# Two graph-attention blocks on one core: x's transposes between the first chunks, and four changed orders

## What is computed

```python
def gat_conv(x, src, dst, W, a_src, a_dst, b, heads, out_ch):
    h = (x @ W).reshape(n, heads, out_ch)
    e = leaky_relu(alpha_src[src] + alpha_dst[dst], 0.2)   # alpha = sum(h * a)
    p = exp(e - segment_max(e, dst)[dst])
    alpha = p / segment_sum(p, dst)[dst]
    return segment_sum(h[src] * alpha, dst) + b
```

## Time and profile before

| what | us |
|---|---|
| median of 3 runs | 380.62 (380.08 to 380.71) |
| the profiled execution, its own time | 379.96 |
| its span | 378.2 |
| PE busy | 357.7 (95%) |
| PEld busy | 306.3 (81%) |
| POOL busy | 248.1 (66%) |
| DVE busy | 218.0 (58%) |
| ACT busy | 214.8 (57%) |
| DMA | 65.15 MB, mean 172 GB/s |

### The profile page before, as it was taken

One profiled execution on the slowest core, in us unless ns is written; L12 is line 12 of the kernel. 1 busy time (PEld: TensorE's weight loads), 2 busy tenths in 40 slices (PEclk: granted clock), 3 DMA queues, 4 the chain that ended last, 5 costly groups with the idle time before them and its releaser, 6 DMA issues.

```text
span 378.2 us, 6192 instructions
## 1 busy us (share of the span) xinstructions
PE 357.7 (95%) x2103; PEld 306.3 (81%) x2106; DVE 218.0 (58%) x563; ACT 214.8 (57%) x374; POOL 248.1 (66%) x171
## 2 busy tenths in 40 slices
PE   6999888999999999999999999998789999899992
PEld 2888787988988988898898898897567888688882
DVE  3697777318236345543741832836665787944866
ACT  4993458756665664773765665564553657245501
POOL 2777707776946948749668686690459876577911
PEclk9999999999999999999999999999999999999998
DMA  7967944637527545754662753755253365355002
GB/s 266 346 193 231 332 196 122 224 124 256 190 87 221 201 160 168 220 194 117 218 240 91 250 170 111 248 184 164 64 188 110 88 179 172 146 168 167 2 0 83
DMA packets 24544, 65.15 MB, mean 172 GB/s; under 512 B 1952, under 2 KB 3024, under 8 KB 24528
## 3 DMA queue, kind: packets, MB, share of 16 engines
q1 hardware_dynamic: 20720, 55.19, 44.4%
q10 hardware_dynamic: 3808, 9.76, 8.1%
HBM read 64.15 MB, written 0.79 MB: 172 GB/s over the span
## 4 chain that ended last, share of the span: by engine, by line
PE 72%; ACT 7%; DVE 6%; issue 6%; POOL 4%; DMA 3%; SPq 1%; POOLq 0%; ACTq 0%; DVEq 0%
PE ps L908 51%; PE ps L1151 8%; PE ps L999 6%; POOL ring_lo L360 3%; ACT ring_hi L347 2%; PE ps L1017 2%; DMA x_sb<-in_x 2%; DMA raw<-in_L_gnn_W 2%; PE ps L972 1%; PE ps L1212 1%; ACT rows_hc L684 1%; POOL x_sb L613 1%; ACT z L684 1%; ACT am L684 1%; PE ps L958 1%
## 5 line engine op out<-in xcount | busy, mean ns | idle before, releaser
L360 POOL TENSOR_TENSOR ring_lo<-raw,ring_hi 128x768 fp32r<-128x768 f32 x94 | 170.8, 1852 | 78.5 <-ACT ring_hi L347 78.5
L347 ACT ACTIVATE ring_hi<-raw 128x768 fp32r<-128x768 f32 x96 | 77.5, 851 | 32.6 <-PE ps L908 28.6
L376 POOL TENSOR_TENSOR ring_lo<-raw,ring_hi 128x512 fp32r<-128x512 f32 (+1 forms) x40 | 59.7, 1523 | 30.6 <-ACT ring_hi L369 30.6
L1341 DVE CUSTOM_DVE_ANT_0 e<-ps,att 128x768 f32<-128x768 f32 (+1 forms) x56 | 41.9, 801 | 53.7 <-PE ps L908 51.1
L908 PE MATMUL ps<-ring_hi,zT_hi 128*128 128x512 f32 (+1 forms) x256 | 69.4, 346 | 1.1 <-DVE zT_lo L1497 1.1
L908 PE MATMUL ps<-ring_hi,zT_lo 128*128 128x512 f32 (+1 forms) x256 | 67.4, 338 | 0.0
L908 PE MATMUL ps<-ring_lo,zT_hi 128*128 128x512 f32 (+1 forms) x256 | 67.3, 338 | 0.0
L908 PE MATMUL ps<-ring_hi,xT_hi 128*128 128x512 f32 x192 | 51.8, 346 | 0.1
L908 PE MATMUL ps<-ring_lo,xT_hi 128*128 128x512 f32 x192 | 51.0, 342 | 0.0
L908 PE MATMUL ps<-ring_hi,xT_lo 128*128 128x512 f32 x192 | 50.6, 340 | 0.0
L908 PEld LDWEIGHTS ps<-ring_lo,zT_hi 128*128 128x128 f32 x256 | 43.1, 188 | 5.7
(11 more groups left out here) (157 smaller groups left out, 554.0 us busy)
## 6 DMA issues: line engine op xcount, KB each, us to landing
raw<-in_L_gnn_W SPq DMA_DIRECT2D x54, 768.0 KB, 4.4
raw<-in_L_gnn_Wr SPq DMA_DIRECT2D x8, 768.0 KB, 4.4
att<-in_L_gnn_a_src ACTq DMA_DIRECT2D x10, 384.0 KB, 4.5
att<-in_L_gnn_a_dst ACTq DMA_DIRECT2D x10, 384.0 KB, 5.5
raw<-in_L_gnn_W SPq DMA_DIRECT2D x4, 384.0 KB, 5.6
x_sb<-in_x SPq DMA_DIRECT2D x3, 256.0 KB, 5.2
rows_hc<-in_L_gnn_b SPq DMA_DIRECT2D x1, 512.0 KB, 5.8
rows_hc<-in_L_gnn_g SPq DMA_DIRECT2D x1, 512.0 KB, 6.7
```

The costliest lines, as they stand in the source:

```text
L347: eng.activation(slot_hi(c), raw_chunk(c), ACT.Copy).then_inc(hi_done, 1)
L360: eng.tensor_tensor(slot_lo(c), raw_chunk(c), slot_hi(c).bitcast(F32), ALU.subtract)\
L376: eng.tensor_tensor(ring_lo[:, q["ring_at"]:q["ring_at"] + w], raw[:, q["raw_group"], q["raw_at"]:q["raw_at"] + w], ring_hi[:, q["ring_at" ...
L1341: dve.tensor_tensor_reduce(junk[:, at:at + w], of[:, (k - first_head(a)) * w:(k - first_head(a) + 1) * w], att[:, half_at * row + k * w:ha ...
```

## The change

It touches all five orders named above. (1) x's parts 1 and 2 are transposed by PE between chunks 0 and 1 and between chunks 1 and 2, and PE's wait for `xT_lo` stands behind them. ACT copies part 1 after it has split chunk 2, and part 2 after the self-loop ramps and the split of chunk 3. DVE writes four hots before `input_lo(1)` and four before `input_lo(2)`. (2) In head 0's ELU the ReLUs of pair 2 come ahead of the high part of pair 1. (3) conv2's exponentials come ahead of the attention loads and of a chunk split, and two idle matmuls are gone. (4) Tile 0 of h1 is centred, scaled and half of it added before tile 1's second statistics. (5) At the end the centring and shift of both tiles come before the first addition.

```diff
@@ act: the opening @@
+            def input_hi(b):
                 act.wait_ge(xT_ps, b + 1)
                 act.activation(xT_hi[:, 2 * b:2 * b + 2, :].rearrange("p k n -> p (k n)"),
                                ps[:, XT_AT + b * BANK:XT_AT + (b + 1) * BANK], ACT.Copy).then_inc(xT_hi_done, 1)
+            split_hi(act, FIRST_PHASE, 0, reused=False)
+            input_hi(0)
+            split_hi(act, FIRST_PHASE, 1, reused=False)
+            split_hi(act, FIRST_PHASE, 2, reused=False)
+            input_hi(1)
             act.wait_ge(iota_cast, 2)
             act.wait_ge(self_cast, 1)
             ramps(ET, ET + NT)
             split_hi(act, FIRST_PHASE, 3, reused=False)
+            input_hi(2)
@@ act: elu(h, hi_first) @@
-                    if q >= 1 and hi_first:
-                        elu_hi(h, q - 1)
+                    if q == 1 and hi_first:
+                        elu_hi(h, 0)
...
-                    if q >= 1 and not hi_first:
+                    if q == 2 or q == 1 and not hi_first:
                         elu_hi(h, q - 1)
@@ act: conv2 @@
             projected_tile_hi(A_CONV2, 1)
+            exps(A_CONV2, (0, 1))
+            chunks_hi(2, 3)
             load_att(A_GAT1A, b1_as1.rearrange("h c -> (h c)"), b1_ad1.rearrange("h c -> (h c)"), HC)
-            chunks_hi(2, 3)
-            exps(A_CONV2, (0, 1))
             weights_tiles_hi(A_CONV2)
@@ pe: the opening @@
+            transpose_x(0)
             for c in range(CH):
-                if c % 2 == 0:
-                    pe.wait_ge(xT_lo_done, c // 2 + 1)
                 if c == 1:
                     pe.wait_ge(b1_loaded, 16)
                     pe.transpose(...)
+                if c in (1, 2):
+                    transpose_x(c)
+                if c % 2 == 0:
+                    pe.wait_ge(xT_lo_done, c // 2 + 1)
                 project_chunk(FIRST_PHASE, 0, c, at=ACC)
@@ pe: conv2 @@
             weights_tiles(A_CONV2)
-            keep_warm(2, idle)
             aggregate(A_CONV2)
@@ dve: the opening @@
             split_lo(dve, FIRST_PHASE, 0)
             input_lo(0)
             split_lo(dve, FIRST_PHASE, 1)
-            input_lo(1)
...
+            hots(0, 4)
+            input_lo(1)
+            hots(4, 8)
             input_lo(2)
...
+            hots(8, ET)
@@ dve: h1 @@
             biased_half(1, 0)
             layer_mean(1, 0, 3 * NT + 1)
-            biased_half(1, 1)
-            layer_mean(1, 1, 3 * NT + 2)
             h1_centre(0, 0)
             h1_centre(1, 0)
             h1_scale(0, 0)
             h1_add(0, 0)
             h1_scale(1, 0)
+            biased_half(1, 1)
+            layer_mean(1, 1, 3 * NT + 2)
+            h1_lo(0, 0)
             h1_centre(0, 1)
-            h1_lo(0, 0)
             h1_centre(1, 1)
             h1_scale(0, 1)
             h1_add(0, 1)
+            h1_add(1, 0)
             h1_scale(1, 1)
-            h1_add(1, 0)
             h1_lo(0, 1)
@@ dve: the end @@
+            out_stats(0)
+            out_centre(0)
+            out_stats(1)
+            out_shift(0)
+            out_centre(1)
+            out_shift(1)
+            for i in range(NT):
                 dve.wait_ge(out_shifted, i + 1)
                 parts = (slice(0, D),) if i == 0 else (slice(N, D), slice(0, N))
```

More of the change, by code:

```diff
@@ L684, in ramps @@
                     act.activation(ramp(t), iota[:, :], ACT.Relu, bias=bias).then_inc(ramp_act_done, 1)
-            split_hi(act, FIRST_PHASE, 0, reused=False)
-            for b in range(3):
+            def input_hi(b):
                 act.wait_ge(xT_ps, b + 1)
@@ L690, in _ @@
                                ps[:, XT_AT + b * BANK:XT_AT + (b + 1) * BANK], ACT.Copy).then_inc(xT_hi_done, 1)
-                if b < 2:
-                    split_hi(act, FIRST_PHASE, b + 1, reused=False)
+            split_hi(act, FIRST_PHASE, 0, reused=False)
[3 more added lines that the diff above has]
+            input_hi(1)
             act.wait_ge(iota_cast, 2)
@@ L1024, in _, with transpose_x @@
             pe.wait_ge(consts, 2)
-            for b in range(3):
+            def transpose_x(b):
                 pe.wait_ge(x_loaded[b], 16)
@@ L1306, in _, with hots @@
             dve.tensor_copy(ident_b, ident[:, :]).then_inc(ident_cast, 1)
+            def hots(first, end):
+                for t in range(first, end):
+                    dve.tensor_scalar(hot(t, 1), iota_ps, edges_f[:, 1, t:t + 1], None, ALU.is_equal)\
+                       .then_inc(hot_done, 1)
+                    if t >= ACT_RAMPS:
+                        dve.tensor_scalar(ramp(t), iota_ps, edges_f[:, 0, t:t + 1], 0.0, ALU.add, ALU.max)\
+                           .then_inc(ramp_dve_done, 1)
             split_lo(dve, FIRST_PHASE, 0)
@@ L1315, in _ @@
                .then_inc(ramp_biased, 1)
+            dve.wait_ge(iota_cast, 1)
+            dve.wait_ge(ramp_biased, 1)
+            hots(0, 4)
+            input_lo(1)
+            hots(4, 8)
             input_lo(2)
@@ L1712, in _, with out_stats, out_centre @@
             nat = [ps[:, GAT2_NAT_AT[i]:GAT2_NAT_AT[i] + D] for i in range(NT)]
-            for i in range(NT):
+            def out_stats(i):
                 dve.wait_ge(nat_done, 3 * NT + i + 1)
                 layer_stats(2, i, nat[i], D)
-            for i in range(NT):
+            def out_centre(i):
                 dve.wait_ge(aggr_done, 2 * NT + i + 1)
@@ L1720, in _, with out_shift @@
                    .then_inc(out_centred, 1)
+            def out_shift(i):
                 dve.wait_ge(out_centred, i + 1)
```

## The result

The changed kernel takes **374.45 us** (median of 4 runs, 374.13 to 377.22) against 380.35 (median of 4, 380.00 to 380.71): a ratio of 0.986, 95% interval 0.9819 to 0.9901. The forecast was 376.0 in a range of 374.7 to 377.9: right in direction, 1.5 us short in size, and as a plain time 0.25 us past the fast end of the range. As a gain it lies on that end: 380.35 - 374.45 = 5.90 us, where the range allowed 380.62 - 374.7 = 5.92. A fifth run, 374.80, is not in that median. Five more runs, taken with the experiments, gave 375.29 (374.05 to 375.61), which is inside the range; the ten together have a median of 374.7.

The account below looks back on a forecast made before the run. PE, with work in 95% of the span, was taken as the bound. Gains of 0.97 + 0.87 + 0.1 + 1.2 + 1.47 = 4.6 us, against the median of 380.62, gave 376.0 us, range 374.7 to 377.9.

Parts of the forecast that it names:

- ELU: Head 0's ELU: exponential, DVE's join and PE's scores come earlier; 0.42 us of PE's 1.29 us wait stay; gain 0.87.
- conv2: conv2: exponentials leave a chunk split and idle matmuls go, but most comes back; gain 0.1, bounds -0.1 and +0.4.
- the split and the issue of two loads now stand between the exponentials and the copies of the transposed weights: conv2, on ACT: this displaced work delays the copies that DVE's low part and PE's aggregation wait for.
- h1: h1: PE's 1.54 us wait at the first transposes goes, 0.3 comes back at tile 1's; gain 1.2.
- The end: Last additions: the small one starts at 371.33 instead of 372.80, with PE the tail's bound; gain 1.47.
- The opening: Start to chunk 5: chunk 0 starts 2.83 us earlier, a new 0.7 us wait on POOL appears; gain 0.97.
- from T2: the copy ... so the split of chunk 4 starts at T2 + 2.12: Opening, on ACT: part 2's copy and four ramps precede chunk 4's split; chunk 4 is ready at T2 + 4.87.
- T2: Opening: the moment when PE has transposed x's part 2, behind chunk 1; forecast at 14.84.
- 4.6 us after the new start: Opening: PE's clock rises to the upper level this long after chunk 0's new start, at 12.06.
- A: Opening gives nothing: the clock rises no earlier, or the next phase loses the microsecond again; 377.0; chance 0.25.
- B: Opening: part of chunk 0 at the upper clock; with half its columns, gain 2.3 and 374.7; chance 0.13.
- Slower (D): Opening: transposes and chunk 4's wait keep PE at the lower clock through the first phase; 385.0; chance 0.03.

Follow-up runs that it names:

- oo_conv2_back: The changed kernel with the opening of before, and conv2's order and two idle matmuls of before as well; 376.53 us (376.21 to 377.26).
- only_open: The kernel before with the new opening alone (its edits on PE, ACT and DVE); 379.41 us (377.72 to 381.40).
- filled: The changed kernel plus three matmuls on zeros between x's first transposes and chunk 0; 374.12 us (373.60 to 374.99).
- a_again: The changed kernel with no edit, for a second profile and more times; 375.29 us (374.05 to 375.61).

## Why the prediction was right and wrong

- **ELU**: forecast 0.87, measured 0.79. The mechanism is as described.
- **conv2**: forecast 0.1, measured 0.18, but the reason was wrong and the size is near by luck. The step "the split and the issue of two loads now stand between the exponentials and the copies of the transposed weights" failed: the loads were issued at 272.43, beside the first exponential, and the copy at 274.69 waited for PE, not for the split. What the change brought is that the exponentials start 0.2 us earlier; before, they stood behind a split, now they wait for their bias. The idle matmuls had cost nothing: the aggregation starts 0.65 us after the last transposes with them (275.20 to 275.85 in oo_conv2_back) and without (275.03 to 275.68).
- **h1**: forecast 1.2, measured 1.18 (1.08 between the first two profiles), with the wait at the second transposes 0.25 where 0.3 was counted.
- **The end**: forecast 1.47, measured 1.48.
- **The opening**: forecast 0.97, measured 0.94 by the medians of only_open and 1.33 on top of the other parts. That the first of these agrees to 0.03 is luck, for two errors stand behind it. The step "from T2: the copy ... so the split of chunk 4 starts at T2 + 2.12" left out ACT's issue of two loads (0.49) and 0.3 to 0.4 of hand-overs: chunk 4 came at T2 + 5.65 to + 5.67, and at + 5.76 in filled, instead of + 4.87, and PE waited 1.2 instead of 0.7 us. Against it stood the clock: "4.6 us after the new start" was right for none of the profiles. T2 was 13.1, 14.1 and 15.6 where 14.84 was forecast, on both sides of it. Rivals A and B were no rivals but executions of one program, which the prediction had called possible.
- **The sum and the range.** The parts measured apart give 0.94 + 3.73 = 4.67, near the forecast's 4.6, and would give 375.7. The changed kernel itself gained 5.06 in the runs taken beside those of the parts, and 5.90 in its first four: 0.4 and 1.2 us more. Its runs go from 374.05 to 377.22 and only_open's over 3.7 us, so a median of four or five can lie a microsecond off; whether something else joins in was not settled. The weak step is the bound: I put B at 0.13 and ended the range at its price, 374.7, when a spread of 0 to 3.1 us in my own bounds for the opening allowed 380.62 - 3.1 - 3.6 = 373.9. That the gain of 5.90 stays within the 5.92 of the range is luck.
- **Slower (D)**: no profile of the new opening kept the lower clock past chunk 1's first pair of matmuls.

## What to carry to other kernels

Ahead of the first long stretch of matmuls, try filling PE's gaps with idle ones: here it took the median from 375.29 to 374.12 among runs taken side by side, and five runs spread over 1.4 us, where ten without it spread over 3.2, one of them far out. When a wait is put on a queue, count everything that the engine issues behind it, DMAs too, and put what the next engine waits for first. A part's worth is read best as a distance between two marks in the profile, since a median of five runs carries the noise of every other stage. And a second profile of the same kernel comes before any story about the first.

## What was not expected of the hardware

- The granted clock of these traces reads 1.00 ahead of the first fall, whatever the level. In the kernel before it reads 1.00 in 10.30:11.30 with matmuls at 1.2 GHz (pairs 0.64 us apart); in a_again it reads 0.54 from 9 to 11 at the same spacing, after an early rise and a fall. In the opening the spacing decides.
- PE's clock rose and fell within 8 us: up before 5.04, down at about 7.44, 0.36 us after a gap of 1.41 us had ended, and up again at 11 (a_again). Behind a gap of the same 1.41 us it stayed up in only_open.
- A DMA issue on ACT's queue runs ahead of activations that precede it in the program (13.32 against 13.79, 272.43 against 273.86), and holds up those behind it (0.49 us).
